# Router of a mixture-of-experts layer: order of the gate, ranking and one-hot steps on ScalarE and VectorE, and gate products in one instruction each

## What is computed

```python
glog = xf @ Wg + bg                                   # 4 groups
ggates, gidx = topk_softmax(glog, 2)                  # 2 of 4 groups
elog = einsum('nd,gde->nge', xf, We) + be             # 8 experts in each group
egates, eidx = topk_softmax(elog, 4)                  # 4 of 8 in each group
combine = gw[:, :, None] * ew                         # product of both gates, 0 where not chosen
y = sum over all 32 experts of combine[:, expert] * (gelu(xf @ W1 + b1) @ W2 + b2)
```

## Time and profile before

| what | value |
|---|---|
| median of 3 runs | 782.56 us (780.7 to 784.25) |
| the profiled execution, its own time | 778.22 us |
| its span in the profile | 776.4 us |
| PE busy | 670.9 us, 86% of the span, 6348 matmuls |
| DVE busy | 424.1 us, 55% |
| POOL busy | 327.2 us, 42% |
| ACT busy | 236.0 us, 30% |
| mean granted clock of PE | 0.906 of 2.4 GHz |
| `norm` of half 1 to the first gather of expert rows | about 340.7 to 388.5 us of the span |
| experts' loop | from about 394 us to the end |

### The profile page before, as it was taken

The page is one execution under the profiler, slowest core; times in us unless marked ns, Lnnn a source line. Parts: engine busy times, 40 slices in busy tenths (PEclk is TensorE's granted clock), DMA queues, the critical chain, the costliest instruction groups (busy, mean ns, idle before and its releaser), DMA issues.

```text
span 776.4 us, 19743 instructions
## 1 busy us (share of the span) xinstructions
PE 670.9 (86%) x6348; PEld 569.6 (73%) x6348; DVE 424.1 (55%) x1247; ACT 236.0 (30%) x673; POOL 327.2 (42%) x265
## 2 busy tenths in 40 slices
PE   5957948898989997863469899999999999999995
PEld 5724736665745985752369899999999999999994
DVE  7675573835579469968833344444444344443442
ACT  3112312123157111113323233333333333333331
POOL 6730820111024222601334466556555555655554
PEclk9968968687999998875589999999999999999998
DMA  9900000000000030031116754564546655465422
GB/s 351 254 7 2 3 3 2 3 2 2 1 1 1 1 123 1 1 133 66 33 39 187 208 163 112 165 167 71 151 108 167 168 163 167 115 169 113 103 47 39
DMA packets 34982, 70.05 MB, mean 90 GB/s; under 512 B 6353, under 2 KB 21234, under 8 KB 34930
## 3 DMA queue, kind: packets, MB, share of 16 engines
q0 software_dynamic: 15840, 17.71, 13.6%
q10 hardware_dynamic: 8064, 33.12, 12.4%
q1 hardware_dynamic: 11026, 18.48, 7.4%
HBM read 59.31 MB, written 9.98 MB: 89 GB/s over the span
## 4 chain that ended last, share of the span: by engine, by line
PE 73%; DVE 13%; issue 6%; POOL 3%; DMA 3%; ACT 1%; DVEq 1%; ACTq 0%; POOLq 0%; SPq 0%
PE bank L1499 18%; PE bank L1491 13%; PE bank L1494 8%; PE bank L1279 4%; PE bank L1347 4%; PE bank L1476 4%; PE bank L1225 3%; PE bank L1381 2%; PE bank L1363 2%; PE bank L1299 2%; PE bank L1317 1%; PE bank L1290 1%; DVE zx L895 1%; DVE arena L935 1%; PE bank L1384 1%
## 5 line engine op out<-in xcount | busy, mean ns | idle before, releaser
L632 POOL DMA_INDIRECT out_dram<-arena,number_u x80 | 127.0, 1587 | 51.8 <-issue 27.4
L626 POOL DMA_INDIRECT arena<-normed_rows,fetch_u x80 | 78.3, 979 | 115.0 <-DMA out_dram<-arena,number_u 49.0
L1186 DVE COPY arena<-bank 128x256 f32<-128x256 f32 x81 | 34.3, 424 | 124.2 <-PE bank L1476 86.6
L797 ACT ACTIVATE arena<-bank,arena 128x128 f32<-128x128 f32 x234 | 64.7, 375 | 115.1 <-PE bank L1494 111.2
L1499 PE MATMUL bank<-arena 128*128 128x192 f32 x468 | 83.2, 326 | 0.0
L1499 PEld LDWEIGHTS bank<-arena 128*128 128x128 f32 x468 | 75.3, 190 | 0.8 <-ACT arena L797 0.8
L1204 DVE TENSOR_SCALAR arena<-bank,arena 128x192 f32 x80 | 33.4, 418 | 62.6 <-PE bank L1499 57.6
L534 POOL TENSOR_SCALAR rstd<-mv 128x4 f32<-128x4 f32 x12 | 2.8, 232 | 141.4 <-DVE mv L884 141.4
L1491 PE MATMUL bank<-arena 128*128 128x128 f32 x468 | 59.2, 276 | 0.4
L1491 PEld LDWEIGHTS bank<-arena 128*128 128x128 f32 x468 | 56.9, 191 | 2.3 <-issue 2.0
L797 ACT ACTIVATE arena<-bank,w_space 128x128 f32<-128x128 f32 x132 | 36.4, 375 | 68.6 <-PE bank L1494 68.6
(11 more groups left out here) (241 smaller groups left out, 1260.2 us busy)
## 6 DMA issues: line engine op xcount, KB each, us to landing
arena<-in_moe_w_dram ACTq DMA_DIRECT2D x14, 579.0 KB
arena<-in_moe_w_dram ACTq DMA_DIRECT2D x14, 576.0 KB
arena<-in_xf_dram SPq DMA_DIRECT2D x8, 512.0 KB, 9.5
w_space<-in_moe_w_dram ACTq DMA_DIRECT2D x7, 579.0 KB
w2small<-in_moe_w_dram ACTq DMA_DIRECT2D x7, 579.0 KB
w_space<-in_moe_w_dram ACTq DMA_DIRECT2D x7, 576.0 KB
wab<-in_moe_w_dram ACTq DMA_DIRECT2D x7, 576.0 KB
arena<-in_w_dram SPq DMA_DIRECT2D x8, 480.0 KB, 8.7
```

What stands on the lines that cost most here:

```text
L626: pool.indirect_dma_start(out=mo_stage[:, s * ROWN:(s + 1) * ROWN], out_offset=None, in_=normed_rows, in_offset=bass.IndirectOffsetOnAxis( ...
L632: pool.indirect_dma_start(out=out, out_offset=bass.IndirectOffsetOnAxis(ap=number_u[:, s:s + 1], axis=0), in_=mo_res[:, s * D:(s + 1) * D] ...
L797: nc.scalar.activation(mo_hT[:, m, :], bank[2 + m][:, 0:P], ACT.Gelu, bias=b1[:, m:m + 1]).then_inc(free[2 + m], 1)
L1186: nc.vector.tensor_copy(mo_xT.rearrange("p k t -> p (k t)"), bank[1][:, 0:2 * P]).then_inc(free[1], 1)
```

## The change

In the list of steps: ranking of the second half stands right behind the gates of the first; `slots` and `begin` of the first half follow the second half's ranking; its one-hot maps become a step of their own, `hot`, behind the second half's gates. On ACT each exponential is issued in the step that makes its input (`rank`, `rank_groups`) and no longer in `gates`, and `number_rows` of the first half goes with `hot`. On DVE the eight products of a half become two. No transfer is added, removed or resized.

```diff
         ("heads_add", "D", 5), ("rank", "R", 0), ("heads_add", "D", 6), ("heads_out", "D", 7), ("heads_add", "D", 7), ("ln", "R", 1),
-        ("rank_groups", "R", 0), ("norm", "R", 1), ("gates", "R", 0), ("slots", "R", 0), ("begin", "R", 0), ("rank", "R", 1),
-        ("rank_groups", "R", 1), ("gates", "R", 1), ("slots", "R", 1), ("counts", "R", 0), ("begin", "R", 1),
+        ("rank_groups", "R", 0), ("norm", "R", 1), ("gates", "R", 0), ("rank", "R", 1), ("rank_groups", "R", 1), ("slots", "R", 0),
+        ("begin", "R", 0), ("gates", "R", 1), ("hot", "R", 0), ("slots", "R", 1), ("counts", "R", 0), ("begin", "R", 1),
         ("table", "R", 0),
...
-            def gate_exps(g):
-                act.wait_ge(sem("gate_shifted"), 2 * g + 1)
-                nc.scalar.activation(gview("E", "d"), gview("E", "d"), ACT.Exp).then_inc(sem("gate_exp"), 1)
-                act.wait_ge(sem("gate_shifted"), 2 * g + 2)
-                nc.scalar.activation(gview("G", "d"), gview("G", "d"), ACT.Exp).then_inc(sem("gate_exp"), 1)
+            def gate_exps(g, which):
+                act.wait_ge(sem("gate_shifted"), 2 * g + (1 if which == "E" else 2))
+                nc.scalar.activation(gview(which, "d"), gview(which, "d"), ACT.Exp).then_inc(sem("gate_exp"), 1)
...
-                elif step_name == "gates":
-                    gate_exps(n)
-                elif step_name == "slots" and n == 0:
+                elif step_name == "rank":
+                    gate_exps(n, "E")
+                elif step_name == "rank_groups":
+                    gate_exps(n, "G")
+                elif step_name == "hot":
                     number_rows(*GROUPS[0])
...
                 for name, dst in (("sel", sel[:, t0:t1, :]), ("d", xrow[:, t0:t1, D:ROWN])):
-                    for q in range(R):
-                        ins = tt(out=dst[:, q, :].rearrange("p (g e) -> p g e", g=G), in0=gview("E", name)[:, q * G:(q + 1) * G, :],
-                                 in1=repeat(gview("G", name)[:, q, :], 2, E), op=ALU.mult)
-                    link(ins)
+                    link(tt(out=dst.rearrange("p t (g e) -> p t g e", g=G), in0=gview("E", name).rearrange("p (t g) e -> p t g e", g=G),
+                            in1=repeat(gview("G", name), 3, E), op=ALU.mult))
...
                 link(nc.vector.tensor_copy(picks_rows[:, t0:t1, :], slots_u[:, t0:t1, :]))
-                if g == 0:
-                    dve.wait_ge(sem("iota_widened"), 1)
-                    rows_hot(t0, t1)
...
+                elif step_name == "hot":
+                    dve.wait_ge(sem("iota_widened"), 1)
+                    rows_hot(*GROUPS[n])
```

## The result

The kernel after took 777.29 us (median of 16 runs, 771.83 to 782.38), the kernel before 781.96 us beside it (16 runs, 776.8 to 784.43). The ratio is 0.9939, 95% interval 0.9916 to 0.9963: between 2.9 and 6.6 us faster. The forecast was 777.7 us, 4.9 us less than before.

What follows compares the result with a forecast made beforehand. The router's string of DVE instructions with holes sets when the PE-busy loop begins. Gains 2.1 + 0.8 + 2.6 + 1.4 less 0.6 and 0.9 give 5.4, less 0.5 is 4.9: 782.56 to 777.7 us, range 773.5 to 780.8.

Steps and rivals of the forecast that it cites:

- Exponentials forward: Before half 0's gates: issuing ACT's exponentials earlier removes DVE's hole of 2.11 us, gain 2.1.
- Products: Router gates on DVE: eight products per half merged into two, gain 0.4 in each half, 0.8 in all.
- Waits for the counts: Before the slots of each half: DVE's wait for PE's count is hidden by other work, gain 1.3 each.
- Logits late: Before half 1's ranking: DVE waits for PE's logits of half 1, loss 0.6 us.
- The adds leave the group rank: Half 1's group rank: two DVE instructions no longer stretched by POOL's residual adds, 0.7 each, gain 1.4.
- a loss of 0.9: Half 1's gates: POOL's first two adds now stretch DVE instructions there, loss 0.9 us, bounds 0 and 1.5.
- a loss of 0.5: Behind half 1's gates: POOL's last two adds come 0.6 us later relative to DVE, loss 0.5, bounds -0.7 and +1.0.
- A: Router: all four POOL adds catch DVE at full length and PE's register reads cost 0.4; gain 3.4, 779.2 us; chance 0.14.
- B: Loop behind the first gather: its 2.9 us of still PE double, leaving a gain of 2.0, 780.6 us; chance 0.08.
- C: Loop start: PE stays at 1.2 GHz for two more tiles, losing 9.2 us; 786.9 us; chance 0.04.
- D: Router: nothing happens because the wait ends late elsewhere; 782.6 us; chance 0.04.

Runs made afterwards that it cites:

- the early maps: Kernel after with the one-hot maps of half 0 moved ahead of half 1's gates; stretch 44.35 us, 778.62 us beside 781.52 for the kernel before.
- the two later profiles of after: Kernel after, unchanged, run twice more against the kernel before: stretch 42.07 and 42.42 us, medians 774.70 and 776.36 us, ratios 0.9928 and 0.9911.

## Why the prediction was right, and where it was off

**What the stretch holds.** The forecast was made of a new schedule of VectorE, so it can be checked mark by mark, in us behind L992 of half 1, foretold and then measured: gates of half 0 start at 1.3 and 1.17; rank of half 1 at 6.0 and 5.88; slots of half 0 at 12.2 and 12.11; gates of half 1 at 14.2 and 14.12; maps at 19.2 and 18.92; slots of half 1 at 21.8 and 21.33; first gather at 42.9 and 41.95. The order of events and each of the holes came as argued. The sum was to be 4.9 and was 5.9.

**The terms.** *Exponentials forward*, 2.1: shown alone, 1.87 with a late PE clock in it and 2.18 without. *Products*, 0.8: shown alone, 0.80; in company 0.5 to 0.6, since the prediction's own next step, the wait for the logits, hides part of half 0's. The prediction had this right in the sum (it booked the 0.6 us of waiting once, behind both) without saying that it makes a part of one term worthless. *Waits for the counts*, 2 x 1.3: both gone, and the early maps bring exactly one back. *Logits late*, a loss of 0.6: 0.56, and 0.67 and 0.70 in the two later profiles of after. *The adds leave the group rank*, 1.4: L975 took 0.23 instead of 0.93 and L977 0.17 instead of 0.94, so 1.47.

**The step that was mis-sized** is POOL's adds, in both places. On the gates I had a loss of 0.9; it was 0.06 + 0.67 = 0.73. For half 1 I took "a loss of 0.5" more; it was 0.04: L1050 lost its whole stretch (-0.67), L1052 kept its own, and the maps took on 0.71. I had named both sides of this, -0.7 and +1.0, as ends of a range and then took a value towards the worse end. The two happen together, so by my own bounds the loss was 0.3, and following the four instructions in order of time, as I did for the gates, would have shown it. I had also not named the instruction that the first of these adds held in before (L1055, 0.86). So 0.46 of the 0.99 us missed (5.89 - 4.9) are those adds behind half 1's gates and 0.17 those on the gates; the rest came in pieces of 0.1 or less.

On the rule of two SBUF inputs, this case's runs agree with the Trainium skill, SBUF — State Buffer, section Who interferes with whom: instructions with two SBUF inputs waited beside an add, the f16 maps among them, which no row of before had shown, while the reduction at 359.53 (0.28) and the reciprocal at 359.85 passed. But two inputs are not the whole condition here: L977 has one tensor input and in before took 0.94 beside an add, where it took 0.17 in half 0. The prediction put it with the others without asking why. That the adds are the cause was inferred until they were taken away; then L1048 took 0.42 and the four maps 2.50.

**The rivals.** A (adds at full length, gain 3.4) fell: they cost less, and PE's register reads cost nothing. B (the loop takes it) has nothing for it in the loop lengths, but what it assumed of the loop was too mild. I had read 2.9 us of still PE as the loop's loss; over twelve profiles the loop ran from 386.9 to 393.8. C (PE's clock) did not occur as told: the twelve matmuls of the first tile took 2.93 us before and after alike, and in the second ten us behind the first gather the clock was 1.00 in both. What the clock did do was to move 0.3 us at the table, to cost a tile in the loop some time behind a long wait, and perhaps to move a part of the 4.4 us ahead of L992. D fell with the holes.

**The total.** 5.9 us of 781.96 would be a ratio of 0.9925. The three measurements of after gave 0.9939, 0.9928 and 0.9911, each interval holding 0.9925. That the measured 4.7 us stood so near the forecast 4.9 is partly luck: the router gave 1.0 more than foretold, and the scatter of the rest took 1.2 away.

## What to carry to other kernels

When a change touches 50 us of 780 and the rest scatters by several, compare the stretch between two marks around the change in both profiles; the equal spans here would have hidden a gain of 5.9 us. In a string of short steps that engines hand to each other, put the other half's independent work behind each handover, and check the queue of every engine: exponentials left in their old place behind a copy cost 1.1 us of what the new order and they can gain together. Before a small piece of work on GpSimd is counted as free, look which VectorE instructions it will meet: here those with two SBUF inputs were held, and one tensor_scalar with a single one.

## What the runs showed that was not expected

PE's clock rises at a different moment of the same matmuls from run to run: the last 16 of the table took 1.16 us in the first profile of after and 1.47 in the third, behind the same work. In the loop it fell once more behind the longest waits of three profiles (3.88, 4.09 and 4.20 us): the next twelve matmuls took 2.93, 2.93 and 2.90 us, where in the first profile of before they took 1.60.

The loop, which looked like 361 us of steady PE, differs by 7 us between profiles of kernels whose loops are the same, through a few waits of up to 4.2 us in its first 100 us and the clock behind them. Followed back, a wait hangs on GpSimd's indirect DMAs that add rows to the output (L632). From 400 to 500 us the chain has one such landing in the first profile of before, 6.78 us long, and three in a row in that of the products alone, 6.46, 6.88 and 6.78 us; there GpSimd waited 4.74 us for one of them ahead of the 4.20 us wait of PE. Why more of them line up in one run than in another was not settled. Between the shortest and the longest loop lie 6.9 us, more than the whole router change.
